# An attention and quantized feed-forward block on one core: score units in pairs, other TensorE work in larger portions, and an opening in another order

## The reference

```
h = layernorm(x)
q = h @ Wq;  k = h @ Wk;  v = h @ Wv
latent = (k + v) @ W_down_kv
k_rec = latent @ W_up_k;  v_rec = latent @ W_up_v
scores = clip(q @ k_rec^T * scale) * exp(-0.0001 * |i - j|)      # per head, 512 x 512
x = x + layernorm(softmax(scores) @ v_rec @ Wo)
xh = layernorm(x) @ Hadamard
xq = round(xh / s) clipped to 4 bits, times s, s = max|xh| / 7 per token
x = x + layernorm(xq @ ternary(weight)^T)
```

## Time and profile before

| | us |
|---|---|
| median of three runs | 1568.07 (1565.24 to 1568.29) |
| the profiled execution | 1565.73 |
| its span, first to last instruction | 1563.8 |
| TensorE busy | 1389.1 (89%) |
| ScalarE busy | 1162.5 (74%) |
| VectorE busy | 1107.5 (71%) |
| GpSimd busy | 911.5 (58%) |

### The profile page before, as it was taken

The page is one execution under the profiler, slowest core; times in us unless marked ns, Lnnn a source line. Parts: engine busy times, 40 slices in busy tenths (PEclk is TensorE's granted clock), DMA queues, the critical chain, the costliest instruction groups (busy, mean ns, idle before and its releaser), DMA issues.

```text
span 1563.8 us, 35962 instructions
## 1 busy us (share of the span) xinstructions
PE 1389.1 (89%) x12330; PEld 587.4 (38%) x12330; DVE 1107.5 (71%) x2604; ACT 1162.5 (74%) x1252; POOL 911.5 (58%) x1188
## 2 busy tenths in 40 slices
PE   5789998999999999999999999999999999999842
PEld 3223333433433343333333433433343343334321
DVE  5547777777777777777777777777777777776643
ACT  0677877878787787878778787877778787778822
POOL 4335665655666665557666655766665566656233
PEclk9899999999999999999999999999999999999975
DMA  5355455455455545645554555555455555545320
GB/s 167 126 156 156 149 170 156 147 177 179 155 162 169 161 150 168 187 149 157 169 171 151 161 185 153 155 168 179 147 157 184 164 156 165 179 144 160 95 66 28
DMA packets 174540, 241.44 MB, mean 154 GB/s; under 512 B 28320, under 2 KB 145184, under 8 KB 174496
## 3 DMA queue, kind: packets, MB, share of 16 engines
q1 hardware_dynamic: 140160, 206.78, 43.2%
q10 hardware_dynamic: 34336, 34.08, 6.7%
HBM read 154.80 MB, written 69.21 MB: 143 GB/s over the span
## 4 chain that ended last, share of the span: by engine, by line
PE 36%; POOL 25%; DVE 14%; issue 8%; DMA 8%; SPq 6%; ACT 1%; POOLq 0%; DVEq 0%
PE heads_ps L641 13%; PE scores_ps L628 8%; SPq L421 6%; DVE ln_stats L1025 5%; PE misc_ps L530 5%; DMA den_spread<-den_scratch 4%; POOL out_sb L976 4%; POOL ln_rstd L928 4%; POOL xn L946 4%; POOL q_hl L967 3%; POOL k_hl L967 3%; DVE x L1100 3%; DMA den_scratch<-den_inv 3%; PE misc_ps L571 2%; POOL k_hl L965 2%
## 5 line engine op out<-in xcount | busy, mean ns | idle before, releaser
L838 ACT ACTIVATE probs<-scores_ps 128x1024 f32<-128x1024 f32 x768 | 777.1, 1025 | 312.1 <-PE scores_ps L628 308.0
L641 PE MATMUL heads_ps<-probs,v_sb 128*32 128x512 f32 x4096 | 533.1, 604 | 36.9 <-ACT probs L845 33.8
L1162 DVE TENSOR_TENSOR diagonal<-scores_ps,comp 128x1024 f32<-128x1024 f32 x256 | 310.6, 1213 | 175.8 <-PE scores_ps L628 175.3
L628 PE MATMUL scores_ps<-q_rep,k_rep 64*128 64x128 f16 (+2 forms) x5120 | 363.1, 252 | 47.1 <-ACT probs L838 27.5
L628 PEld LDWEIGHTS scores_ps<-q_rep,k_rep 64*128 64x128 f16 x5120 | 157.1, 94 | 505.9 <-issue 279.3
L845 ACT ACTIVATE probs<-diagonal 128x2048 f32<-128x2048 f32 x128 | 243.9, 1906 | 0.0
L972 POOL TENSOR_TENSOR heads_c<-heads_c,den_spread 128x1024 f32<-128x1024 f32 x32 | 75.7, 2366 | 231.6 <-DMA den_spread<-den_scratch 231.6
L1079 DVE SCALAR_TENSOR_TENSOR weighted<-misc_ps,edges 128x384 f32<-128x384 f32 x256 | 130.3, 551 | 66.7 <-PE misc_ps L541 66.3
L921 POOL TENSOR_TENSOR ln_neg_mean<-zero,ln_moments 128x4 f32<-128x4 f32 x128 | 37.9, 296 | 208.6 <-DVE ln_moments L1033 208.6
L641 PEld LDWEIGHTS heads_ps<-probs,v_sb 128*32 128x32 f32 x4096 | 87.8, 108 | 174.7 <-issue 145.7
L965 POOL TENSOR_TENSOR q_hl<-weighted,zero 128x768 f16<-128x768 f32 x64 | 94.3, 1473 | 92.7 <-DVE weighted L1079 92.7
(11 more groups left out here) (110 smaller groups left out, 1555.2 us busy)
## 6 DMA issues: line engine op xcount, KB each, us to landing
q_rep<-q_scratch SPq DMA_DIRECT2D x128, 384.0 KB, 3.8
k_rep<-k_scratch SPq DMA_DIRECT2D x256, 192.0 KB, 4.4
q_scratch<-q_hl SPq DMA_DIRECT2D x64, 384.0 KB, 2.3
k_scratch<-k_hl SPq DMA_DIRECT2D x64, 384.0 KB, 3.0
x_in<-in_L_attn_x_dram ACTq DMA_DIRECT2D x32, 512.0 KB, 3.6
heads_c<-heads SPq DMA_DIRECT2D x256, 64.0 KB, 2.3
x_res<-in_L_attn_x_dram ACTq DMA_DIRECT2D x32, 512.0 KB, 4.9
den_spread<-den_scratch SPq DMA_DIRECT2D x256, 64.0 KB, 2.4
```

The costliest lines, as they stand in the source:

```text
L628: ins = mm(scores_ps[:, place + par, at:at + n * P], k_rep[rows, pair, kv_, k_cols], q_rep[rows, pair, qv_, q_cols], start=True, stop=True)
L641: ins = mm(heads_ps[W32 * g:W32 * (g + 1), :], v_sb[:, b.slot, kt, at:at + W32], probs[:, quad % 2, g, kt, :], start=(kt == 0), stop=(kt = ...
L838: nc.scalar.activation(flat[:, :, at:at + S], scores_ps[:, place:place + 2, :], ACT.Exp, scale=EXP_SCALE).then_inc(off_probs, 1)
L1162: v.tensor_tensor(diagonal[:, quad % 2, 2 * two:2 * two + 2, :], scores_ps[:, place:place + 2, :], comp[:].rearrange("p t n -> p (t n)").u ...
```

## The change

The three step tables and the lists of GpSimd and SyncE are new. On TensorE most score units now stand in pairs, with the other stages between the pairs. xT, x1T and xh do both parts in a row, pv's portions are grouped, q's second half stands around the first piece of y, and z's two parts stand one behind unit 0 and one behind unit 1. The waits of `spread` are for q first and for k after q's two DMAs, which needs two semaphores for the stores. SyncE compacts the heads before it packs the denominators. In the opening TensorE turns the ternary weights and takes the norms before v, VectorE builds the ternary weights behind the first half of k, the tables are a function of their own (`diagonal_tables`) ahead of `path_choice`, and v is taken out after `fast_ok` is set. Some instructions of a batch change place; none is added or removed in the steady loop.

```diff
 TENSOR_STEPS = {
-    0: [("z", 0, 0), ("z", 1, 0)], 2: [("pv_end", 3, 0), ("pv_end", 3, 1), ("pv_end", 3, 2)], 4: [("xT", 0, 0)], 5: [("xT", 1, 0)],
...
+    0: [("z", 0, 0)], 1: [("z", 1, 0), ("pv_end", 3, 0), ("pv_end", 3, 1)], 3: [("pv_end", 3, 2)], 5: [("xT", 0, 0), ("xT", 1, 0)],
...
 SCALAR_STEPS = {
-    7: [("load_res", 0), ("z_apply", 0), ("z_apply", 1)], 11: [("z_apply", 2), ("x1T", 0)],
...
+    5: [("load_res", 0)], 9: [("z_apply", 0)], 11: [("z_apply", 1), ("z_apply", 2)], 12: [("x1T", 0)], 13: [("x1T", 1)],
+    14: [("load_x", 0)], 22: [("z_apply", 3), ("round_x", 0), ("round_x", 1)], 23: [("round_x", 2), ("round_x", 3)], 29: [("qintT", 0)],
...
-POOL_STEPS = ["rstd4", "x1_apply", ("q", 0), ("k", 0), "heads_normalize", ("k", 1), "add_out", "x_apply", ("q", 1), "rstd2"]
+POOL_STEPS = ["rstd4", "x1_apply", ("q", 0), ("k", 0), "heads_normalize", ("k", 1), "add_out", ("q", 1), "x_apply", "rstd2"]
...
             def spread(b, c):
...
-                sp.wait_ge(qk_stored[c], 16 * STORES * (b.number + 1))
+                sp.wait_ge(q_stored[c], 16 * (b.number + 1))
...
+                sp.wait_ge(k_stored[c], 16 * (b.number + 1))
+                for again in range(2):
...
...
         @block.tensor
...
             def opening_batch(b):
...
                 k_stage(b, 0, 0)
+                up_weights(0, w_up_k)
+                up_weights(1, w_up_v)
                 k_stage(b, 1, 0)
-                up_weights()
-                v_stage(b, 0, 0)
+                turn_ternary()
                 for piece in range(2):
                     q_stage(b, 1, piece)
                 weight_norms()
-                turn_ternary()
+                v_stage(b, 0, 0)
...
         @block.vector
...
             def opening_batch(b):
...
-                ternary_weights()
                 dve.wait_ge(second_loaded, 16 * SECOND)
                 weigh(b, "q", 0)
                 lat_take(b, 0)
                 weigh(b, "k", 0)
+                ternary_weights()
                 weigh(b, "k", 1)
+                take_ternary()
+                diagonal_tables()
+                weigh(b, "q", 1)
+                x_stats(b.other(1))
+                x_moments(b.other(1))
+                path_choice()
                 for part in range(2):
                     v_take(b, part)
-                x_stats(b.other(1))
-                x_moments(b.other(1))
-                weigh(b, "q", 1)
-                path_choice()
```

More of the change, by code:

```diff
@@ L67 @@
 TENSOR_STEPS = {
[6 rows of a table removed]
[6 rows of a table added]
 }
 SCALAR_STEPS = {
-    7: [("load_res", 0), ("z_apply", 0), ("z_apply", 1)], 11: [("z_apply", 2), ("x1T", 0)],
-    13: [("x1T", 1), ("load_x", 0), ("z_apply", 3)], 20: [("round_x", 0)], 22: [("round_x", 1)], 26: [("round_x", 2), ("round_x", 3)],
-    31: [("qintT", 0)],
+    5: [("load_res", 0)], 9: [("z_apply", 0)], 11: [("z_apply", 1), ("z_apply", 2)], 12: [("x1T", 0)], 13: [("x1T", 1)],
+    14: [("load_x", 0)], 22: [("z_apply", 3), ("round_x", 0), ("round_x", 1)], 23: [("round_x", 2), ("round_x", 3)], 29: [("qintT", 0)],
@@ L87 @@
-POOL_STEPS = ["rstd4", "x1_apply", ("q", 0), ("k", 0), "heads_normalize", ("k", 1), "add_out", "x_apply", ("q", 1), "rstd2"]
-SYNC_STEPS = [("own", "spread", 1), ("a", "gather_den"), ("a", "pack_den"), ("a", "compact", 1), ("a", "return_den"),
-              ("pre", "store_q", 0), ("pre", "store_k", 0), ("a", "spread_den"), ("pre", "spread", 0), ("own", "compact", 0),
-              ("pre", "store_q", 1), ("pre", "store_k", 1), ("c", "store_out")]
+    0: [("z", 0), ("z", 1)], 1: [("x1_make",)], 3: [("z_stats",)],
@@ L92 @@
+SYNC_STEPS = [("own", "spread", 1), ("a", "gather_den"), ("a", "compact", 1), ("a", "pack_den"), ("a", "return_den"),
+              ("a", "spread_den"), ("pre", "store_k", 0), ("pre", "store_q", 0), ("pre", "spread", 0), ("pre", "store_k", 1),
+              ("pre", "store_q", 1), ("own", "compact", 0), ("c", "store_out")]
 ORDER_ALL = [step for h in sorted(TENSOR_STEPS) for step in TENSOR_STEPS[h] if step[0] in PARTS]
@@ L476, in general_path @@
                 for c in range(DC):
[L477 removed]
+                    sp.wait_ge(q_stored[c], 16)
+                    sp.wait_ge(k_stored[c], 16)
                 with sp.Fori(0, B) as i:
@@ L691, in latent_weights, with up_weights @@
                 ins.then_inc(setup_pe, 1)
-            def up_weights():
-                pe.wait_ge(second_loaded, 16 * SECOND)
-                pe.wait_ge(setup_dve, 3)
-                for w, up in enumerate((w_up_k, w_up_v)):
-                    for ci in range(DC):
-                        ins = mm(scores_ps[:, 2 + w, ci * D:(ci + 1) * D], w_latT[:, ci * P:(ci + 1) * P], up[0:LAT, :], start=True, stop=True)
+            def up_weights(w, up):
+                for ci in range(DC):
+                    ins = mm(scores_ps[:, 2 + w, ci * D:(ci + 1) * D], w_latT[:, ci * P:(ci + 1) * P], up[0:LAT, :], start=True, stop=True)
                 ins.then_inc(setup_pe, 1)
@@ L991, in opening_batch @@
                 x_apply(b)
-                for name, c in SPLITS[:3]:
+                for name, c in SPLITS:
                     split(b, name, c)
                 x_apply(b.other(1))
-                split(b, *SPLITS[3])
             opening_batch(Batch(0, 0, 2))
```

50 lines of the change are left out of this document (25 added, 25 removed), and 10 rows, old and new, of the table TENSOR_STEPS.

## The result

| | us | against before, 95% interval |
|---|---|---|
| before, median | 1568.18 | |
| changed kernel, median of four runs | 1500.32 (1498.96 to 1502.66) | 0.9567 [0.9541, 0.9592] |
| its profiled execution, and its span | 1498.96, 1497.1 | |
| forecast | 1489, range 1470 to 1526 | |

What follows compares the result with a forecast made beforehand. TensorE was taken as the bound. Opening minus 6, batches 0 to 3 minus 8, batches 4 to 30 minus 62.6, batch 31 minus 3, drain 0: together minus 79.6, forecast 1489 us, range 1470 to 1526.

Steps and rivals of the forecast that it cites:

- additive costs: TensorE's work priced per portion plus an entry cost of 0.10 to 0.20 us; larger portions were to save 0.6 a batch.
- Unit 5: Score unit behind units 2 and 3 and one pv portion; TensorE was to wait 0.66 us for ScalarE's exp 3.
- x1T: TensorE was to wait 0.74 us there for GpSimd's normalized x1, its own chain having become shorter.
- k: TensorE was to wait 0.24 us until VectorE, following ScalarE's copies, had taken both banks of x1T.
- The old ones at z and at the last quad's pv: TensorE's waits of 0.58 us before z and 1.12 before the last quad's pv were to be gone.
- that v would not wait: The old 0.29 us wait before v was to vanish, VectorE having weighted k by then.
- The walk: One period of the new order followed with every engine in its own order, using reaction times; result 43.07 us.
- Rival B: Slower: denominators' chain, den_packed issued behind compacting, landing late and holding k's second half, v, y; 1584 us, chance 0.05.
- The opening: Set-up before the first unit 0: minus 6 us, between minus 3 and minus 8, unit 0 near 38.5.
- Batches 0 to 3, batch 31 and the drain: Batches 0 to 3 minus 8 us, batch 31 minus 3, drain 0 plus or minus 2.
- Rivals A and D: A: ScalarE's waits grow back, 1521 us, chance 0.13; D: waits at x1T and k vanish, 1465 us, chance 0.06.
- (c): The forecast's new wait of 0.74 us at x1T, for GpSimd's normalized x1.

Runs made afterwards that it cites:

- e13: Changed kernel with denominators packed first, plus xh's two halves and the three pv portions in a row taken apart again; 1516.31 us, ratio to before 0.9676.

## Why the prediction was right, and where it was off

**Costs of the work: right.** The merged rows took what the additive costs say: two pv portions from 775.52 to 777.38, 1.86; x1T 1.03; xh, from 798.30 to 800.15, 1.85. e13 confirms the size (0.46 by starts). One part was off to the good: q, y and q take 2.78 where the additive costs say 3.18, and y in front of qintT 0.97 for 1.06, together 0.49 a batch. In the period shown the work is 41.00, against 41.35 forecast and 41.95 in before.

**Waits: three of four as forecast.** Unit 5: 0.66 forecast, 0.67 measured. Unit 10: 0.08 and 0.12. x1T: 0.74 and 0.60. k: 0.24 and 0.04. The old ones at z and at the last quad's pv are gone, as said. With v's all waits are 2.51, where before had 3.4 and the forecast 1.72. (The forecast's list of the waits of before leaves out one of 0.34 in front of unit 17, longer than two that it names; its sum goes by starts and doesn't need the list.)

**The step that failed: that v would not wait.** Its wait is 1.08 us. The walk itself held (packing issued at 13.75 after unit 2 forecast, 13.82 measured). Rival B said that v is met if the landing comes within 3 us of the issue, and I let that stand in the forecast as given. The row of before had 2.7, with the packing ahead of the compacting, and I kept it where the change puts it behind four other DMAs: it took 3.8 to 3.9. The rival's condition, its place and its direction were right; its price at the landing that came, 0.9 us late, was 1.08 a batch or 29 us, and it belonged in the sum as a term with a range instead of a rival with one end. In the period shown, 43.51 against 43.07, the 0.44 too much are 1.08 for v and some 0.2 of work and small waits, less 0.49 (q and y) and 0.34 (x1T and k). Over batches 4 to 30 the gain missed by 0.31, 2.01 instead of 2.32, since before's mean there was 45.44 and not 45.39. That the total came so near is in part luck: an unforecast 29 us were offset by 22 us that had been put too high.

**The opening: the term was mis-sized.** 2.1 instead of 6, and 1.8 on the means of several profiles. The order came out as forecast (tables early, the choice of path 3.9 us from 37.22 to 41.10, 1.3 before unit 0), but the choice began 3.7 us later than the 33.5 forecast: I took VectorE's durations from a place where GpSimd rested, and the ternary weights took 2.8 more and the decay tables 1.9.

**Batches 0 to 3, batch 31 and the drain** came within 1.3 us of their terms. The clock did stay at its lower level for less time: from 40.8 to 54.4 in before, 13.6 us, and from 40.0 to 50.2 in the changed kernel. Rivals A and D did not come: no wait of ScalarE's appeared at units 12, 23 or 24, and (c) stayed.

## What to carry to other kernels

When a transfer is moved behind others in its queue, its landing time is a new number, not the old one; ask what engine stands in order behind its consumer, and keep that consumer out of the middle of work that others wait for. Merge TensorE's portions of one kind, since each entry between score units and the rest costs 0.10 to 0.20 us here and a short portion leaves the other engines behind. And test an edit with the chain that sets the period in place and without it: the pv portions gave 0.46 a batch with v's wait there and 0.13 without, z's moments 0.24 and 0.25, the first time by a shorter landing and the second by x1T's wait. What an edit gives in one kernel is no price for the next.
